# One gate matmul per token tile, weights split and set up later, and the first batch's gathers without clearings between them

## The chip, the cores and the metric

The kernel runs on one core of one Trainium2 chip. The metric is the time of one execution on the device in microseconds; for a kernel several executions are taken and their median is given. The engines are TensorE (PE; its weight loads are shown as PEld), VectorE (DVE), ScalarE (ACT), GpSimd (POOL) and SyncE (SP), each with its own in-order queue of instructions, tied together by semaphores.

## The reference

For each of 16 images `x[b]` (64 channels, 128x128) and texts `txt[b]` (128 tokens of 64):

```python
q_feat = bilinear_sample(x, 32x32 grid)                      # 1024 queries
queries = q_feat @ W_q.T
off = gelu(layer_norm(q_feat @ W_o1 + b_o1)) @ W_o2 + b_o2   # 8 points a query
sampled = bilinear_sample(x, grid + 4 * off * scale)         # 1024 x 8 points, 4 corners each
h = softmax(q . (sampled @ W_k.T)) over the 8 points, applied to sampled @ W_v.T
h = concat([h, txt])                                         # 1152 tokens of 64
h = h + ssm(layernorm(h))       # diagonal complex recurrence over the BATCH index, 16 steps
z = layernorm(h)
logits = z @ gate_w + gate_b ; top 2 of 16 experts, softmax over the two
h = h + sum_e dispatch[e] * ((silu(z @ w1[e]) * (z @ w2[e])) @ w3[e])   # 16 experts, hidden 128
```

All 16 experts are computed for every token, and the dispatch weight of the experts not chosen is zero. Because the recurrence runs over the batch, batch b+1 needs the state of batch b.

## The kernel before

Each batch passes through three stages, and the stages of neighbouring batches overlap:

- **Map** (pieces A1 to B6). SP loads the image in 8 units; PE transposes it (A1, 16 pieces, L770), ACT copies it to `pixmaj` (L913), and SP writes it in four quarters (Q) to a table in HBM, in rows of 2 pixels by 64 channels. A2 (L783) samples the regular grid, A3 and B0 make the queries, B1 to B5 the offsets, and B6 on DVE the table indices `idx` and the corner weights `cw`. B1 needs one power on POOL (L616).
- **Gather** (G on POOL, then D1 to D5 and S1 to S3). A batch has 8 tiles of 128 queries with 8 points each, so 64 indirect gathers, in 32 units `G` of two (L601). A unit ends with a clearing of a scratch tile `rest` (L608). Two gather buffers alternate, so tile j may be gathered once tile j-2 was weighted. D1 (DVE, L1138) multiplies half a tile by the corner weights, D2 (PE, L748) sums the corners by transposing into one bank, ACT copies, D3 (PE, L758) projects to keys and values, DVE multiplies by the queries and reduces. S1 to S3 are the softmax over four tiles (`u` = 0, 1), with the large product at L1166 and three additions at L1173.
- **FFN** (P1 to P9, R, X, W, Z, M2), in three groups of 384 tokens. P1 and P5 are the layernorms (a power on POOL each, L621 and L624), P2 to P4 the recurrence step, P6 makes the transposed token tile `xsplit`, P7 the gate: logits (PE, L736), on DVE bias (L1100), maxima and indices, P8 the dispatch weights, P9 turns them. R spreads an expert pair's weight over the bank (PE, L694). X is an expert's two hidden products (PE, L658 and L659, two passes each, high and low part of the weight), silu on ACT (L842) and the product on DVE (L1038). W is the third weight (L667), scaled on DVE (L1045), and Z sums (L677).

The order of pieces on each engine is written out by hand as strings (`ORDER`), one letter a piece; every engine walks its string and waits in it. So a piece that is early in its data still waits for the pieces in front of it on its engine. Batch 0's FFN starts while the last tiles of batch 0 are gathered.

**Set-up.** SP loads 42 constants in four parts between image units 2 to 5 (`load_constants`). Among them are w3 (L554) and w1 and w2, each twice (four loads of 512 KB), into the two gather buffers as scratch. Before its first piece DVE waits for all of them, splits w1 and w2 into a high and a low part (L960, L961), then waits for four exponentials of ACT (`setup`, which ACT runs after its last map copy of batch 0), computes phases (L974 to L986), and signals `setup_done`. PE waits for that before A2 of batch 0, and POOL before its first gather. The 128x64 transposition of `b_st` (L640), its copy (L830), a sine on ACT (L832) and the rotation matrix (L989 to L991) follow; they are needed first by P2 and P3.

Of the kernel before, what the change touches and what calls it, by code (L numbers as in the profile page):

```python
# [34 lines left out]
C = 64  # L35
# [21 lines left out]
RESTS = 1  # L57
# [23 lines left out]
def grid():  # L81
# [99 lines left out]
        "DlDJIDmDJmtJluJIvJlJImJKmxJIlJzaJlIJmaBJmIDaJDlDJIDalDJaDmJDKDItmJuaJlIaJlvIJamJbmbJIbbJbbxbJKIblJzI",
        "lJcmJBmJIDdDJlDJIDeDlDJKDmDJItmJuJlIJlvhJiImJamJaIJxaJKIJzaIJaaJJaaIBJDJDIlDJKDJIDlDJmDJIDmtJluJIvJl",
        "JImJKmxJIlJzaJlIJmaBJmIDaJDlDJIDalDJaDmJDKDItmJuaJlIaJlvIJamJbmbJIbbbJbxbJKIblJzIlJcmJBmJIDdDJlDJIDe",
        "DlDJmDJKDItmJuJlIJvlhJIimJImJaJxaJaKIJzIaJaJaJaIaBJDJDIDlDJKDJIDlDJmDJItmuJlvJIJlJImJxmJKIlJzaJlIJma",
        "BJmIDaJDlDJIDalDJaDmJDKDItmJuaJlIaJlvIJamJbmbJIbbbJbxbJKIblJzIlJcmJBmJIDdDJlDJIDeDlDJmDJKDItmJuJlIJl",
        "vhJiImJamJaIJxaJKIJzaIJaaJJaaIBJDJDIlDJKDJIDlDJmDJIDmtJluJvIJlJImJKmxJIlJzaJlIJmaBJmIDaJDlIDJaDlJDam",
        "DJKDIDmtJauJlIaJlvIJamJbmbJIbbbJbxbJKIblJzIlJcmJBmJIDdDJlDJIDeDlDJmDJKDItmJuJlIJlvhJiImJamJaIJxaJKIJ",
        "zaIJaJaJaaIBJDJDIlDJKDJIDlDJmDJIDmtJluJIvJlJImJKmxJIlJzaJlIJmaBJmIDaJDlDIDJaDlJDamDJKDItmJuaJlIaJlvI",
        "JamJbmbJIbbbJbxbJKIblJzIlJcmJBmJIDdDJlDJIDeDlDJKDmDJItmJuJlIJlvhJiImJamJaIJxaJKIJzaIJaJaJaaIBJDJDIDl",
        "DJKDJIDlDJmDJItmuJlvJIJlJImJKmxJIlJzaJlIJmaBJmIDaJDlDJIDalDJaDmJDKDItmJuaJlIaJlvIJamJbmbJIbbbJbxbJKI",  # L190
        "blJzIlJcmJBmJIDdDJlDJIDeDlDJmDJKDItmJuJlIJlvhJiImJamJaIJxaJKIJzaIJaJaJaaIBJDJDIDlDJKDJIDlDJmDJItmuJl",
        "vJIJlJImJKmxJIlJzaJlIJmaBJmIDaJDlDJIDalDJaDmJDKDItmJuaJlIaJlvIJamJbmbJIbbbJbxbJKIblJzIlJcmJBmJIDdDJl",
        "DJIDeDlDJKDmDJItmJuJlIJlvhJiImJamJaIJxaJKIJzaIJaaJJaaIBJDJDIlDJKDJIDlDJmDJIDmtJluJIvJlJImJKmxJIlJzaJ",
        "lIJmaBJmIDaJDlDIDJaDlJDamDJKDItmJuaJlIaJlvIJamJbmbJIbbbJbxbJKIblJzIlJcmJBmJIDdDJlDJIDeDlDJmDJKDItmJu",
        "JlIJvlhJIimJImJJxJKIJzIJJJIBJDJDIlDJKDJIDlDJmDJIDmtJluJIvJlJImJKmxJIlJzIJlJmJIBmDJlDJIDlDJmDJKDIDmDJ",
        "ItJluJlvIJmJmJIJxJKIlJzIlJmJmJIBJlDJIDlDJmDJKDIDmDJlDJItJluJIvmJImJKJxIJzJJIJJIBJDJDIJDKDJIDJIDJDJDI",
        "tJuJIvJKJIJxJIzJJIJBJDJDIJDKDJIDJIDJDJDItJuJIvJKJIxJJzIJJIJBJDIDJKDJIDJDJDIDJDJIJJIJKJIJJIJJIJIK",
    ),
    "act": (
        "aaaaaaaaaaaaaaaabcdghaaaaaaaalmmaaalammlmamaaablcmdmEglmhmsltamumaawaalxamJmzJaJaBaDJDJaDJlDmDJmDJaD",  # L200
        "JEDJaJalamJsmJJtulJwmJmxJzJaJBaslDJmDJmDJDJDJDJlDJmDmtJuEJwlbJmcJmdxJzlJmBJsmDJDDJDDJDlDJmDJgtmuJhJw",
        "JlJmamaJxaJEJaJaJzaJaaBJDsJDDDJDJDlDJmDJtmuJJJwlJmJxmJJaJzlJmaBJmDsaDJDDJaDlJDamDJDtmJuaJEaJlJamwJmJ",
# [55 lines left out]
        "oosoooooowoooooosoowswsw",  # L258
    ),
    "sp": (  # L260
        "ppHHppCppCppCppCppCppCppCppCpppppCCpCppCrHrppCppCrppCrpHpCrppCppCrppCrpHpCrppCppCrppCrpHpCrppCppCrpp",
        "CrpHpCrppCppCrppCrpHpCrppCppCrppCrpHpCrppCppCrppCrpHpCrppCppCrppCrpHpCrppCppCrppCrpHpCrppCppCrppCrpH",
        "pCrppCppCrppCrpHpCrppCppCrppCrpHpCrppCppCrppCrHCrrrrrrrr",
    ),
# [970 lines left out]
OFF_READ = 12  # L1235
SOFT_N = 7
LN_N = 2
TOP_N = 12


# [48 lines left out]
```

## Time and profile before

| | us |
|---|---|
| median of 3 runs | 2207.96 (2207.76 to 2212.83) |
| the profiled execution | 2205.73 |
| its span | 2203.9 |
| PE busy in the span | 2028.7 (92%) |
| DVE busy | 1775.4 (81%) |
| POOL busy | 1513.4 (69%) |
| ACT busy | 1184.9 (54%) |
| mean granted clock of TensorE | 0.977 |

The profile is that of one execution; its own time is 2205.73 us, and the runs of the table's first line are others. The share of busy time of an engine is a mean over stages with different limits. In the slices of the page PE is at 2 to 8 tenths in the first four of 40 slices (55 us each) and at 9 in nearly all that follow.

### The profile page before, as it was taken

The numbers are of one execution on the slowest core, as the hardware profiler recorded it, in microseconds if no ns is written. First come the engines' busy times: TensorE is split into PE (matmuls) and PEld (weight loads), VectorE is DVE, ScalarE is ACT, GpSimd is POOL, SyncE is SP. The second block draws the span as 40 slices with busy tenths as digits, with TensorE's granted clock in tenths as the row PEclk, the third lists the DMA queues.
The fourth block names the chain that finished last, engine by engine and source line by source line (L and its number), as shares of the span: only waits on it lengthen the run. The fifth ranks groups of instructions, "written<-read, shape, count | busy, mean of one in ns | idle before, by whom it ended". The sixth has DMA issues, their size and how long they took to land.

```text
span 2203.9 us, 42639 instructions
## 1 busy us (share of the span) xinstructions
PE 2028.7 (92%) x13857; PEld 1541.3 (70%) x13857; DVE 1775.4 (81%) x4292; ACT 1184.9 (54%) x3048; POOL 1513.4 (69%) x1753
## 2 busy tenths in 40 slices
PE   2468999999999999999999999999999999999998
PEld 1346677777777777777777777777777677776765
DVE  1346788888889888888988888898988889898875
ACT  1225555555565555655555565555556556654553
POOL 0378778778686867868676786868688686868700
PEclk9778999999999999999999999999999999999999
DMA  8786726667654656656464666646476664632200
GB/s 196 218 240 171 214 74 186 178 179 197 168 156 116 188 161 186 195 165 174 121 192 133 188 197 172 184 121 194 119 201 176 179 191 126 184 95 75 71 3 6
DMA packets 363274, 346.61 MB, mean 157 GB/s; under 512 B 49456, under 2 KB 313776, under 8 KB 362928
## 3 DMA queue, kind: packets, MB, share of 16 engines
q1 hardware_dynamic: 313904, 209.60, 34.9%
q0 software_dynamic: 49152, 134.28, 21.0%
q8 instruction: 114, 1.87, 0.4%
q14 instruction: 104, 0.85, 0.1%
HBM read 205.90 MB, written 137.89 MB: 156 GB/s over the span
## 4 chain that ended last, share of the span: by engine, by line
PE 67%; DVE 12%; POOL 10%; issue 8%; ACT 2%; DMA 1%; POOLq 0%; DVEq 0%; ACTq 0%; SPq 0%
PE bank_h L658 11%; PE bank_o L667 10%; PE bank_h L659 9%; PE bank_d L748 9%; PE bank_d L758 9%; POOL gath L601 7%; PE bank_z L677 4%; PE bank_p L694 4%; PE bank_a L770 2%; DVE hid L1038 2%; DVE v_sb L1166 2%; DVE v_sb L1173 2%; PE bank_p L713 2%; PE bank_p L718 1%; POOL rest L608 1%
## 5 line engine op out<-in xcount | busy, mean ns | idle before, releaser
L601 POOL DMA_INDIRECT gath<-table,idx x1024 | 1133.9, 1107 | 258.5 <-issue 239.8
L658 PE MATMUL bank_h<-xsplit,w 128*128 128x384 f32 x1536 | 587.5, 382 | 18.7 <-DVE hid L1038 17.5
L659 PE MATMUL bank_h<-xsplit,w 128*128 128x384 f32 x1536 | 521.1, 339 | 0.0
L842 ACT ACTIVATE silu<-bank_h 128x384 f32<-128x384 f32 x768 | 382.5, 498 | 241.7 <-PE bank_h L659 239.7
L1038 DVE TENSOR_TENSOR hid<-silu,bank_h 128x384 f32<-128x384 f32 x768 | 419.9, 550 | 82.0 <-ACT silu L842 74.0
L658 PEld LDWEIGHTS bank_h<-xsplit,w 128*128 128x128 f32 x1536 | 293.0, 191 | 118.8 <-issue 63.8
L1138 DVE TENSOR_TENSOR wsam<-gath,cw 128x1024 f32<-128x1024 f32 x256 | 313.0, 1223 | 53.0 <-PE bank_d L748 27.0
L667 PE MATMUL bank_o<-hid,w_sb 128*64 128x384 f32 x1536 | 334.7, 514 | 12.2 <-DVE scaled L1045 10.8
L748 PE MATMUL bank_d<-eye,wsam 128*128 128x128 f32 x2048 | 275.7, 279 | 25.3 <-DVE wsam L1138 24.8
L659 PEld LDWEIGHTS bank_h<-xsplit,w 128*128 128x128 f32 x1536 | 293.7, 191 | 3.2
L758 PE MATMUL bank_d<-w_kv,samT 128*128 128x256 f32 x1024 | 278.5, 395 | 5.6 <-ACT v_sb L898 2.7
L748 PEld LDWEIGHTS bank_d<-eye,wsam 128*128 128x128 f32 x2048 | 237.5, 143 | 63.0 <-DVE wsam L1138 41.9
L882 ACT COPY wide<-bank_p 128x384 f32<-128x384 f32 x384 | 185.0, 482 | 161.8 <-PE bank_p L694 161.2
L770 PE MATMUL bank_a<-eye,xin 128*128 128x128 f32 x1024 | 171.4, 294 | 76.9 <-DMA xin<-x_dram 43.4
L621 POOL TENSOR_SCALAR lns<-lns 128x3 f32<-128x3 f32 x96 | 39.1, 408 | 293.4 <-ACT lnsq L848 289.4
L913 ACT COPY pixmaj<-bank_a 128x512 f32<-128x512 f32 x256 | 150.2, 587 | 139.9 <-PE bank_a L770 137.6
L1045 DVE TENSOR_TENSOR scaled<-bank_o,wide 128x384 f32<-128x384 f32 x384 | 212.2, 553 | 12.2 <-PE bank_o L667 8.1
L758 PEld LDWEIGHTS bank_d<-w_kv,samT 128*128 128x128 f32 x1024 | 181.3, 193 | 51.8 <-issue 22.1
L608 POOL MEMSET rest<- 1x400 f32 x512 | 215.9, 422 | 0.2
L770 PEld LDWEIGHTS bank_a<-eye,xin 128*128 128x128 f32 x1024 | 127.2, 149 | 114.7 <-issue 56.3
L1144 DVE TENSOR_TENSOR k_sb<-k_sb,q_sb 128x256 f32<-128x256 f32 x256 | 108.3, 423 | 114.8 <-ACT v_sb L898 114.0
L894 ACT COPY k_sb<-bank_d 128x256 f32<-128x256 f32 x256 | 95.3, 372 | 156.1 <-PE bank_d L758 155.0
(157 smaller groups left out, 2704.4 us busy)
## 6 DMA issues: line engine op xcount, KB each, us to landing
table<-pixmaj SPq DMA_DIRECT2D x80, 1024.0 KB, 9.7
xin<-x_dram SPq DMA_DIRECT2D x256, 256.0 KB
table<-pixmaj SPq DMA_DIRECT2D x32, 960.0 KB
table<-pixmaj SPq DMA_DIRECT2D x16, 1088.0 KB
gath<-table,idx POOLq DMA_INDIRECT x1024
out_dram<-ob SPq DMA_DIRECT2D x48, 96.0 KB, 7.0
gath<-w_dram SPq DMA_DIRECT2D x4, 512.0 KB, 9.5
interp_sb<-interp_dram SPq DMA_DIRECT2D x1, 1024.0 KB, 5.2
```

Of the source, the lines that this page charges most:

```text
L601: pool.indirect_dma_start(out=gath[buf][:, p, :, :].rearrange("p a c -> p (a c)"), out_offset=None, in_=table[par], in_offset=bass.Indirec ...
L608: nc.gpsimd.memset(rest[:], 0.0).then_inc(rested, 1)
L658: mm(bank[:, 0:GC], w12[:, e, which, 0, :], xsplit[gp][:], start=True, stop=False)
L659: mm(bank[:, 0:GC], w12[:, e, which, 1, :], xsplit[gp][:], start=False, stop=True).then_inc(ready, 1)
L667: last = mm(bank_o[C * h:C * (h + 1), 0:GC], w3_sb[:, 2 * q + h, :], hid[:, (2 * n + h) % HB, :], start=True, stop=True)
L748: last = mm(bank_d[:, 128 * (2 * f + pair):128 * (2 * f + pair + 1)], wsam[:, corner, 2 * pair:2 * pair + 2, :].rearrange("p n c -> p (n c)"),
L758: last = mm(bank_d[:, 256 * i:256 * (i + 1)], samT[:, 2 * f + i, :], w_kv[:], start=True, stop=True)
L770: last = mm(bank_a[:, 128 * r:128 * (r + 1)], xin[u % 2][:, HW * (4 * (c % 2) + r):HW * (4 * (c % 2) + r + 1)], eye[:], start=True, stop=T ...
L842: nc.scalar.activation(silu[e % 2][:], bank_h[r][:, 0:GC], ACT.Silu).then_inc(silu_done, 1)
L1038: tt(hid[:, n % HB, :], silu[e % 2][:], bank_h[r][:, 0:GC], ALU.mult).then_inc(hid_done, 1)
L1045: tt(scaled[n % SB][:], bank_o[:, 0:GC], wide[:, q, :], ALU.mult).then_inc(eo_scaled, 1)
L1138: tt(wsam[:].rearrange("p a n c -> p n a c"), gath[j % GB][:, 4 * f:4 * f + 4, :, :], spread(w, 3, C), ALU.mult).then_inc(weighted, 1)
```

## The change

Four things are changed, and the order strings with them (2896, 2240, 2480, 624 and 256 pieces on PE, ACT, DVE, POOL and SP as before; the set of pieces is the same).

1. **Gate.** `gate_r` holds the high and the low part of the gate weights. Before, a token tile was multiplied by each with 16 columns, the second adding into the bank (6 matmuls a group). Now it is multiplied once by both, side by side (3 matmuls of 32 columns), and DVE adds the two halves in an instruction of its own.
2. **Weights.** w3 and the raw w1 and w2 are no longer among the constants. SP issues them (7 loads) right behind the last table quarter of batch 0, into the FFN tiles `wide` and `hid`; w2 is split in two halves. DVE splits them in three steps (`split_weights`) in front of D1 pieces (1,1), (2,0) and (2,1) of batch 0. The constants are now 37 in four parts.
3. **Set-up.** ACT runs the exponentials after its first samples copy (D2 of tile 0), the g_in copy and the sine after that of tile 1; DVE computes the phases in front of D1 (1,0) and the rotation in front of D1 (3,0); PE transposes `b_st` in front of D2 (1,1). A2 waits for the constants alone, and the first gather no longer for `setup_done`.
4. **Gathers.** A unit of batch 0 ends without clearing `rest`; the units of the other batches clear it as before.

Order: POOL's string begins with B1 and all 32 units of batch 0 with P1 of group 0 in front of the last; then B1 of batch 1, the first unit of batch 1, P5 of group 0. Before, B1 of batch 1 stood after unit 20, P1 after 25 and P5 after 29. On DVE S1 and S2 of the last tiles now stand in front of P6n, and S3 in front of P6 of group 0; before, they stood nine expert products later. On PE all D2 and D3 of batch 0 stand in front of the first expert, before two of its tiles' pieces stood behind it. Later batches differ in single swaps.

```diff
     "pool": (
-        "eooooooooooooooooooooeooooosoooowooooooooooooosooowoooosooooooowooooosooeooowooooooosooooowoooooosoooo",
...
+        "eooooooooooooooooooooooooooooooosoeowoooosoooooowooooosooooooowoooooosooeowooooooosoooooowoooooosooo",
...
-            (gate_f[0:C, :], gate_w), (gate_f[C:128, :], gate_w), (w3_sb[:], w3.rearrange("e h o -> h e o")),
+            (gate_f[0:C, :], gate_w), (gate_f[C:128, :], gate_w),
...
-        raw_w = [gath[0][:].rearrange("p a b c -> p (a b c)"), gath[1][:].rearrange("p a b c -> p (a b c)")]
+        flat = wide[:].rearrange("p a b -> p (a b)")
+        raw_w = [(0, 0, NE, flat[:, 0:NE * HID]), (1, 0, NE // 2, flat[:, NE * HID:NE * HID * 3 // 2]),
+                 (1, NE // 2, NE, hid[:].rearrange("p a b -> p (a b)")[:, 0:NE // 2 * HID])]
...
-            loads += [(dst, src, raw_in) for dst, src in raw_loads]
...
                         table_quarter(b, par, args[0])
+                        if b == 0 and args[0] == 3:
+                            for dst, src in raw_loads:
+                                sp.dma_start(dst, src).then_inc(raw_in, 16)
...
-                if k == 0 and b == 0:
-                    pool.wait_ge(setup_done, 1)
...
-                for n in range(RESTS * (4 * QT * b + k), RESTS * (4 * QT * b + k + 1)):
+                if b > 0:
+                    n = 4 * QT * (b - 1) + k
                     wait(pool, rested, n)
                     nc.gpsimd.memset(rest[:], 0.0).then_inc(rested, 1)
...
+                        if n == 0:
+                            pe.wait_ge(split_v, 2 * len(raw_w))
...
+                        if n == 0:
+                            pe.wait_ge(raw_in, 16 * (2 * len(raw_w) + 1))
...
-                            for part in range(2):
-                                last = mm(bank_p[:, NE * k:NE * (k + 1)], xsplit[gp][:, 128 * k:128 * (k + 1)],
-                                          gate_r[:, part, :], start=part == 0, stop=part == 1)
+                            last = mm(bank_p[:, 2 * NE * k:2 * NE * (k + 1)], xsplit[gp][:, 128 * k:128 * (k + 1)],
+                                      gate_r[:].rearrange("p a e -> p (a e)"), start=True, stop=True)
...
+                        if b == 0 and (j, f) == (1, 1):
+                            setup()
...
-                                setup()
+                                pe.wait_ge(const_in, N_CONST)
...
+                        if b == 0 and j == 0:
+                            setup()
+                        if b == 0 and j == 1:
+                            setup_state()
...
+            def split_weights(n):
+
+                which, first, last, raw = raw_w[n]
+                raw = raw.rearrange("p (e h) -> p e h", h=HID)
+                high = w12[:, first:last, which, 0, :]
+                if n == 0:
+                    dve.wait_ge(raw_in, 16 * (2 * len(raw_w) + 1))
+                vcopy(high, raw).then_inc(split_v, 1)
+                dve.wait_ge(split_v, 2 * n + 1)
+                tt(w12[:, first:last, which, 1, :], raw, high.bitcast(F32), ALU.subtract).then_inc(split_v, 1)
...
-                        link(top, tt(logit[:], bank_p[:, 0:GT * NE].rearrange("p (k e) -> p k e", k=GT),
-                                     spread(gateb[:], 1, GT), ALU.add))
+                        parts = bank_p[:, 0:2 * GT * NE].rearrange("p (k a e) -> p k a e", k=GT, a=2)
+                        link(top, tt(logit[:], parts[:, :, 0, :], spread(gateb[:], 1, GT), ALU.add))
+                        link(top, tt(logit[:], parts[:, :, 1, :], logit[:], ALU.add))
...
+                        if b == 0:
+                            if (j, f) == (1, 0):
+                                setup_phases()
+                            elif (j, f) == (3, 0):
+                                setup_rot()
+                            elif (j, f) in ((1, 1), (2, 0), (2, 1)):
+                                split_weights(2 * j + f - 3)
```

## Rows read from the trace of the kernel before

**Rows 1.** Stretches: window, length, busy PE, PEld, DVE, ACT, POOL, clock, DMA.

```profile
196.20:335.10 138.90, 128.65 (x870) 96.58 (x869) 116.81 (x279) 78.64 (x202) 107.54 (x128) 0.99 0.59 165
462.40:1988.60 1526.20, 1481.49 (x10369) 1138.53 (x10368) 1318.38 (x3193) 881.38 (x2274) 1137.95 (x1309) 0.99 0.59 167
```

**Rows 2.** What PE waited for, 335.1 to 1988.6 us: total, times, longest.

```profile
PE bank_a L770 <- ACT pixmaj L913: 13.0, 17, 0.8
PE bank_h L658 <- DVE hid L1038: 12.1, 28, 1.7
PE bank_p L684 <- DVE dispr L1127: 10.1, 12, 0.9
```

**Rows 3.** SP's issues in order of time: start, length, engine, line, what.

```profile
11.56 0.59 SPq L554 DMA_DIRECT2D w_sb<-w_dram  x1
12.19 2.23 SPq L554 DMA_DIRECT2D b_st<-bmat_dram  x1
...
24.22 2.93 SPq L554 DMA_DIRECT2D d_row<-dvec_dram  x1
27.19 7.40 SPq L554 DMA_DIRECT2D gath<-w_dram  x4
34.63 4.27 SPq L554 DMA_DIRECT2D w_off<-w_o_dram  x5
...
68.67 4.62 SPq L534 DMA_DIRECT2D table<-pixmaj  x2
91.64 1.12 SPq L519 DMA_DIRECT2D xin<-x_dram  x2
```

**Rows 4.** The set-up chain to the first gather, in order of time.

```profile
67.53 0.58 ACT L913 COPY pixmaj<-bank_a 128x512 f32<-128x512 f32 x1 [1.27 <-PE bank_a L770]
...
68.59 0.23 DVE L974 TENSOR_SCALAR col<-col 128x2 f32<-128x2 f32 x1 [8.20 <-ACT col L828]
...
71.94 3.23 PE L783 MATMUL bank_a<-pixmaj,interp_sb 128*32 128x64 f32 x128
...
82.36 1.65 POOL L616 TENSOR_TENSOR off_s<-off_s,neghalf 128x8 f32<-128x8 f32 x1 [80.78 <-DVE off_s L1189]
...
90.56 1.24 POOL L601 DMA_INDIRECT gath<-table,idx  x1 [6.56 <-DVE idx L1218]
```

**Rows 5.** DMA engines from 75 to 92 us: busy tenths, 39 slices.

```profile
DMA  9999998310000000000000000000000000000000
```

**Rows 6.** POOL: groups from 90.5 to 199.3 us, then single instructions.

```profile
L601 POOL DMA_INDIRECT gath<-table,idx x64 | 69.8, 1091 | 21.4 <-issue 14.7 <-DVE idx L1218 6.6 <-DVE wsam L1138 0.2
L608 POOL MEMSET rest<- 1x400 f32 x32 | 13.5, 422 | 0.0
...
93.64 0.95 POOL L601 DMA_INDIRECT gath<-table,idx  x1 [0.16 <-issue]
94.89 0.94 POOL L601 DMA_INDIRECT gath<-table,idx  x1 [0.30 <-issue]
...
155.68 1.68 POOL L616 TENSOR_TENSOR off_s<-off_s,neghalf 128x8 f32<-128x8 f32 x1 [6.03 <-DVE off_s L1189]
...
199.86 0.95 POOL L601 DMA_INDIRECT gath<-table,idx  x1 [0.16 <-issue]
```

**Rows 7.** A gather beside a DVE product, and the weight split's operations.

```profile
161.22 2.23 DVE L1166 TENSOR_TENSOR v_sb<-v_sb,score 128x2048 f32<-128x2048 f32 x1
161.68 2.58 POOL L601 DMA_INDIRECT gath<-table,idx  x1 [0.30 <-issue]
...
49.72 1.23 DVE L960 CAST w<-gath 128x2048 fp32r<-128x2048 f32 x1
50.98 2.29 DVE L961 TENSOR_TENSOR w<-gath,w 128x2048 fp32r<-128x2048 f32 x1
```

**Rows 8.** First silu; and the chain from D2 of the last tile to S3.

```profile
196.81 0.49 ACT L842 ACTIVATE silu<-bank_h 128x384 f32<-128x384 f32 x1
...
206.63 0.87 PE bank_d L748 x8
...
223.47 0.43 DVE v_sb L1173
```

**Rows 9.** Gate matmuls from 462.4 to 1988.6 us; the bias addition, whole span.

```profile
L736 PE MATMUL bank_p<-gate_r,xsplit 128*128 128x16 f32 x216 | 26.3, 242 | 0.0
...
L1100 DVE TENSOR_TENSOR logit<-bank_p,gateb 128x48 f32<-128x48 f32 x48 | 9.7, 202 | 2.2 <-PE bank_p L736 2.1
```

More of the change, by code:

```diff
@@ L194 @@
[L194 to L197, printed above, removed]
+        "aaaaaaaaaaaaaaaabbbbbbbbcdehiaaaallamamaallmmalaaalmmllmmlalamamabbbbbbbblcdlemmllmmltuvhilammaaaxaa",
@@ L410, in build @@
         raw_in = sem("raw_in")
+        split_v = sem("split_v")
         setup_v = sem("setup_v")
@@ L540, in out_group @@
                              ob[gp][:]).then_inc(out_done[gp], 16)
-            raw_loads = [(raw_w[n][C * half:C * (half + 1), :].rearrange("c (e h) -> c e h", e=NE),
-                          w.rearrange("e c h -> c e h")) for n, w in enumerate((w1, w2)) for half in range(2)]
+            raw_loads = [(raw[C * half:C * (half + 1), :].rearrange("c (e h) -> c e h", h=HID),
+                          (w1, w2)[which][first:last].rearrange("e c h -> c e h"))
+                         for which, first, last, raw in raw_w for half in range(2)]
+            raw_loads.append((w3_sb[:], w3.rearrange("e h o -> h e o")))
             loads = [(dst, src, const_in) for dst, src in const_loads]
-            loads += [(dst, src, raw_in) for dst, src in raw_loads]
             loads += [(dst, src, const_in) for dst, src in block_loads]
@@ L955, in _ @@
             step(nc.vector.memset(state[:], 0.0))
-            dve.wait_ge(raw_in, 64)
-            for n in range(2):
-                raw = raw_w[n].rearrange("p (e h) -> p e h", e=NE)
-                step(vcopy(w12[:, :, n, 0, :], raw))
-                step(tt(w12[:, :, n, 1, :], raw, w12[:, :, n, 0, :].bitcast(F32), ALU.subtract))
             step(vcopy(sel[:].rearrange("p (e c) -> p e c", c=C), spread(lnsq[:, 0, 0:NE], 2, C)))
@@ L979, in _ @@
-            for op, sign in ((ALU.is_gt, -1.0), (ALU.is_lt, 1.0)):
-                step(ts(col[:, 18:20], col[:, 16:18], -sign * PI, sign * TWO_PI, op, ALU.mult))
-                step(tt(col[:, 16:18], col[:, 16:18], col[:, 18:20], ALU.add))
-            step(ts(col[:, 16:18], col[:, 16:18], -PI, PI, ALU.max, ALU.min))
-            assert su.n == PHASES_READY
-            step(tt(col[:, 8:9], col[:, 6:7], col[:, 12:13], ALU.mult))
-            step(ts(b_st[:], b_st[:], col[:, 6:7], None, ALU.mult))
@@ L1112, in run @@
                         g = args[0]
-                        top.start(b, TOP_N * g + 4)
+                        top.start(b, TOP_N * g + 5)
                         dve.wait_ge(gap_tanh, NGRP * b + g + 1)
@@ L1228, in _ @@
             run()
-PHASES_READY = 29
-SETUP_V = 35
+PHASES_READY = 25
+SETUP_V = 31
 OFF_N = 20
@@ L1237 @@
 LN_N = 2
-TOP_N = 12
+TOP_N = 13
 def kernel(**inputs):
```

203 lines of the change are left out of this document (106 added, 97 removed).

## The prediction

> **What bounds the kernel now.** The views were read in this order: busy shares by stretch, PE's waits, SP's queue at the start, the chain of set-up, then POOL. In [rows 1] the reader is to see two regimes. From 462.4 to 1988.6 us PE is busy for 1481.5 of 1526.2 us, at the full granted clock but for short stretches; these are twelve batches, counted from one's last silu to another's, of 127.2 us each. There a microsecond of PE work removed is worth up to a microsecond, and the 2.9% of idle time is mostly PE waiting for DVE results or map copies [rows 2]. Before 196 us PE is mostly idle: it waits for the map, the table and the gathers of batch 0. There only the chain SP, then set-up, then POOL counts, up to the first expert matmul at about 195 us (its silu starts at 196.81 [rows 8]).
>
> **1. Earlier loads: -9.8 us on the map's arrival.** SP issues without a pause until its last table quarter, so what leaves its queue moves everything behind it. Out go the w3 load (0.59), the four raw weight loads (7.40), and what the 2.23 us of b_st exceeds an ordinary load by, since it stands right behind w3's small packets (2.23 - 0.5 = 1.7) [rows 3]: 9.7, with one w_off load moved a quarter earlier and gamma a quarter later making about nothing by the sixth unit; I take 9.8. Ends: if raw's 7.40 us was mostly SP held back by the table quarter before it, only 4 x 0.6 = 2.4 of it is work, and the gain is 2.4 + 0.6 + 1.7 = 4.7 us. If in turn the w_off loads (4.27 for five, 0.85 each) were held back by raw, it is 12 us. What moves: seven loads (2.5 MB) are now issued behind quarter 3, which ends at 68.67 + 4.62 = 73.3; SP's next issue waited until 91.64 [rows 3]. At 1.85 us each (7.40/4) they take 13 us of that gap of 18, so they delay nothing; without that cover x units 2 and 3 of batch 1 would be late by the overshoot, and no gather. They land before DVE asks for them at its fourth product, some 15 us after the gathers begin.
>
> **2. Set-up off the chain: -3.8 us.** In [rows 4] DVE stands idle until ACT's exponentials at 68.59, then works through the phases, and PE's A2 starts only at 71.94. ACT's last map copy ends at about 68.1 (67.53 + 0.58, and the exponentials follow right on it), so A2 may start at 68.1: 3.8 us. The small projections and B6 behind it are untouched and end in the first gather at 90.56. The moved pieces cost DVE some 4 us (14 small operations of 0.17 to 0.25) and ACT a Sin table load, inside the gather phase of batch 0, where DVE is about half idle and the gathers run two tiles ahead of it; I cost them at nothing, at most 3 us if DVE becomes late for a gather buffer. The first gather thus comes at 90.6 - 9.8 - 3.8 = 77.0 us. The table is not late: the DMA engines fall quiet by 80 us [rows 5], some 10 before the first gather, and that point moves by 9.8 against 13.6.
>
> **3. POOL's phase of batch 0.** Today the 64 gathers take from 90.56 to 199.3 [rows 6]. The 32 clearings look like 13.5 us, but the gap in front of a gather is 0.16 after a clearing and 0.30 after a gather, so a unit goes from 0.95 + 0.30 + 0.95 + 0.42 + 0.16 = 2.78 to 2 x (0.95 + 0.30) = 2.50: 0.28 x 32 = 9.0 us. The order also changes: B1 of batch 1, for which POOL stood idle 6.03 us and worked 1.7 (8 us), now follows the last gather, and only P1 of group 0 remains inside (1.6 us; P5, 2.4 us, moves out).
>
> Against it stands a loss. A gather normally takes 0.95 us; some of the 64 take longer, 9.0 us in all (69.8 - 64 x 0.95), and in [rows 7] one that starts inside DVE's 2.23 us product lasts 2.58 and ends 0.8 us after it. The six weight splits that the change puts between D1 pieces last 1.23 + 2.29 + as much again in halves = 7.0 us [rows 7]. A gather waits on average for what is left of the operation beyond its own place in the 1.25 us rhythm; I take 4 us, between 0 (if every split falls between two gathers) and 7.0. That makes 80.0 + 1.6 + 9 + 4 = 94.6 us, so the last gather ends at 171.6, 28 us earlier than now.
>
> The Trainium skill, "SBUF — State Buffer", section "Who interferes with whom", says that a DVE operation with two inputs in SBUF and a GpSimd instruction that reads SBUF shut each other out for the whole instruction, and that one that only writes (the clearing) is not held. The trace agrees on both: 2.58 us beside 2.23 for a gather, and clearings at a mean of 422 ns throughout [rows 6, 7]. By it the splits would cost up to their 7 us, 3 more than my sum.
>
> **4. But the first expert matmul gains almost nothing.** POOL's order now makes the chain serial. Behind the last gather stand B1 (0.3 + 8.2 us from B1 to the gather that needs its result, as 82.36 to 90.56 [rows 4]), and one D1 of 1.2 in the middle of it: batch 1's gathers start at 181.5, 18 us earlier than 199.9 [rows 6]. P5 of group 0 stands behind them. On DVE, P6 of group 0 now stands behind D1, S1, S2 and S3 of the last tiles. From D2 of that tile to the end of S3 the chain today takes 206.63 to 223.9 = 17.3 us [rows 8]. The last D2 starts at 171.6 + 6.7 (B1, B2 and B4, then D1 of 1.2), S3 ends at 195.6, P6 and the gate add 1.0: the first expert matmul at 196.6, against about 195.1. So 28 us on POOL turn into -1.5 us here.
>
> What the delay buys: D3 of tile 6 and all of D2/D3 of tile 7 lie before the first expert matmul now, some 5.3 us of PE work (five pieces; a D2 is 0.87 [rows 8], and I estimate a D3, whose four matmuls are twice as wide, at a fifth more), and the gathers of batch 1 are 18 us ahead, so of PE's 10.3 idle us between 196.2 and 335.1 [rows 1], half of which waits on weighted samples, I take 5 as gone. Sum of the beginning: 9.8 and 3.8 and the rest have gone into POOL's lead, and what the end sees is -1.5 + 5.3 + 5.0 = 8.8 us. It ranges from -4 (every late term at its bad end: 5 us less at SP, 3 at POOL, 5.0 not gained) to 25 (S1 to S3 in 12 us as DVE is freer, loads 12 us).
>
> **5. One-pass gate: -9.6 us.** The six matmuls of a group occupy PE for 26.3 us/216 = 0.122 us each [rows 9]; 48 groups lose three each: 144 x 0.122 = 17.5 us if 32 columns cost no more than 16. The nearest row is weight loads of the same 128x128 shape, which set this rhythm and are halved; at the other end, a matmul twice as long would leave 0. DVE gains 48 additions of the size of L1100 (0.20 us [rows 9] and 0.03 of hand-over): 11 us on an engine that is busy 86% of this stretch. PE waits for the dispatch 12 times and for hidden products 28 times in 39 groups [rows 2]; there the added 0.23 us eats most of the 0.37. I take 0.20 kept per group, 9.6 us; range -3 to 17.5. Other moves in the order strings (B0 a few places later, single swaps) I cost at nothing, +-2.
>
> **Sum.** The profiled execution took 2205.7 us (span 2203.9 and 1.8 around it). 8.8 + 9.6 = 18.4: 2187.3. The median of the runs is 2208.0, 2.3 above the profiled one, so the forecast for a median is 2189.6, as **2189 us**.
>
> **Rivals.**
> - *The lead survives.* DVE, freed of the FFN's early pieces, gets through D1 to S3 faster, or PE fills the gap; the end sees 18 of POOL's 28 us, and the gate brings 15: 2208 - 33 = 2175. For it: PE's idle share before 196 us is the largest reserve. Against it: the fixed order on POOL and DVE.
> - *The gate gives nothing.* The chain through DVE (addition, maxima, indices, P8, dispatch) sets the pace, or 32 columns cost double; only the beginning counts: 2208 - 9 = 2199. For it: the DVE waits in [rows 2]. Against: they are 2% of the stretch.
> - *Little of either.* 2205.
> - *Slower: the first FFN starts late.* Place: POOL's queue, B1 and P5 of batch 0 behind all 32 units, and P6 behind S3. Price: each microsecond of lateness of the last gather is one of the whole. Decides from a first expert matmul at 195.1 + 5.3 + 5 + 9.6 = 215 us on. It needs SP's gain at its low end (5), the splits at 7, and gathers that wait for late D1 pieces (10): 196.6 + 5 + 3 + 10 = 214.6, and the gate at its bad end: 2208 + 9 = 2217.
>
> **Chances.** Forecast 0.50 (own range 2181 to 2197), lead survives 0.20, gate gives nothing 0.16, little of either 0.08, slower 0.06. The range 2171 to 2203 leaves out the slower case and part of the next. The chance of being faster by over 0.3% (below 2201.4; 0.3% is about what a measurement of this kernel tells from no change) is 0.86, within it 0.08, slower 0.06.
>
> **What would show it.** First gather near 77 us and A2 right behind the last map copy (steps 1, 2); gather rhythm 2.50 us and the last one near 172 (3); longer gathers beside the splits; batch 1's gathers near 181 and the first silu near 198 (4); L736's successor with 144 matmuls, and a period between silus of one batch and the next of 126.5 instead of 127.1 (5). A first silu before 190 or after 208, or a period unchanged to 0.1 us, would prove me wrong.

## The result, and the profile after

| | before | after |
|---|---|---|
| median, 5 runs each | 2207.96 us (2206.97 to 2213.07) | 2193.04 us (2188.33 to 2194.95) |
| profiled execution | 2205.73, span 2203.9 | 2190.43, span 2188.6 |
| mean granted clock in it | 0.977 | 0.969 |

The ratio of the two is 0.992, 95% interval 0.9902 to 0.9939: faster by 0.8%, 14.9 us by the medians and 15.3 us by the profiled executions. The forecast was 2189 us, range 2171 to 2203. In every ratio of this document an execution that took over 1.5% longer than the fastest of its kernel is left out as a slow one (in this comparison there is none).

Where the 15.3 us arose is read from the start of the last silu of each batch. That of batch 0 comes at 322.6 instead of 335.1 us (-12.5), of batch 12 at 1844.9 instead of 1861.7 (-16.8), of batch 13 at 1971.1 instead of 1988.6 (-17.5), of batch 15 at 2181.3 instead of 2196.6 (-15.3). So most of it is won by the end of batch 0, a few us in the steady batches, and 2 us are lost again at the end.

The busy shares by stretch, with the columns of [rows 1]: the phase of the first gathers, the stretch up to the first expert matmul, batch 0's FFN, and the same twelve batches as before, from the last silu of batch 1 to that of batch 13.

```profile
75.40:166.20 90.80, 55.71 (x376) 42.36 (x377) 47.72 (x79) 26.92 (x66) 71.50 (x67) 0.73 0.87 239
166.20:196.30 30.10, 21.32 (x72) 14.15 (x72) 19.62 (x44) 8.63 (x25) 13.34 (x14) 0.56 0.30 72
196.30:322.60 126.30, 120.76 (x838) 92.77 (x839) 104.60 (x272) 74.53 (x193) 96.55 (x113) 0.99 0.61 172
449.40:1971.10 1521.70, 1475.05 (x10262) 1127.50 (x10261) 1319.14 (x3229) 881.12 (x2275) 1138.84 (x1309) 0.99 0.60 167
```

Against [rows 1] batch 0's FFN has 7.9 us less PE work (128.65 to 120.76) and 4.8 us less idle (10.3 to 5.5). By the rows of single lines in the same windows, 16 of D2's and 12 of D3's matmuls have gone from it (20.26 to 17.79 and 20.48 to 17.05 us, together 5.9), and half of the gate's (2.40 to 1.45). The twelve batches take 1521.7 us where they took 1526.2: 126.8 against 127.2 a batch. PE's work fell by 6.4 us and its idle time rose by 1.9. What it waited for from the end of batch 0 on (322.6 to 1971.1 us, thirteen batches; total, times, longest), against [rows 2]: the hidden product now comes first, and the wait for map copies has grown from 13.0 to 16.9 us.

```profile
PE bank_h L665 <- DVE hid L1064: 17.5, 24, 1.7
PE bank_a L780 <- ACT pixmaj L930: 16.9, 22, 0.8
PE bank_p L693 <- DVE dispr L1154: 7.7, 10, 0.9
```

SP's queue, against [rows 3]: start and length of each issue.

```profile
11.55 0.59 SPq L557 DMA_DIRECT2D b_st<-bmat_dram  x1
...
16.84 3.11 SPq L536 DMA_DIRECT2D table<-pixmaj  x2
19.99 4.53 SPq L557 DMA_DIRECT2D col<-gamma_dram  x2
24.56 0.59 SPq L557 DMA_DIRECT2D d_row<-dvec_dram  x1
25.20 2.74 SPq L557 DMA_DIRECT2D w_off<-w_o_dram  x6
...
57.16 4.72 SPq L536 DMA_DIRECT2D table<-pixmaj  x2
61.93 6.92 SPq L572 DMA_DIRECT2D wide<-w_dram  x4
68.91 3.02 SPq L572 DMA_DIRECT2D hid<-w_dram  x2
71.97 1.23 SPq L572 DMA_DIRECT2D w_sb<-w_dram  x1
76.51 2.19 SPq L521 DMA_DIRECT2D xin<-x_dram  x2
```

The last table quarter is issued at 57.16 instead of 68.67, 11.5 us earlier. b_st costs 0.59 instead of 2.23 us, six w_off loads 2.74 where five took 4.27, but two tiny gamma loads behind a table quarter 4.53. The seven late loads end at 73.2, before SP's next issue at 76.51.

The set-up chain, against [rows 4]: A2 (L793) begins right behind the last map copy, and the first gather at 75.43 instead of 90.56.

```profile
56.02 0.59 ACT L930 COPY pixmaj<-bank_a 128x512 f32<-128x512 f32 x1 [1.27 <-PE bank_a L780]
...
56.75 3.32 PE L793 MATMUL bank_a<-pixmaj,interp_sb 128*32 128x64 f32 x128 [0.77 <-ACT pixmaj L930]
...
67.21 1.66 POOL L621 TENSOR_TENSOR off_s<-off_s,neghalf 128x8 f32<-128x8 f32 x1 [65.64 <-DVE off_s L1223]
...
75.43 1.24 POOL L605 DMA_INDIRECT gath<-table,idx  x1 [6.56 <-DVE idx L1252]
```

In the gather phase, the first step of the weight split on DVE (its two operations, L1017 and L1019) and the gathers beside it, against [rows 7]:

```profile
103.33 1.22 DVE L1017 CAST w<-wide 128x2048 fp32r<-128x2048 f32 x1
104.58 2.29 DVE L1019 TENSOR_TENSOR w<-wide,w 128x2048 fp32r<-128x2048 f32 x1
106.79 1.22 DVE L1172 TENSOR_TENSOR wsam<-gath,cw 128x1024 f32<-128x1024 f32 x1
```

```profile
102.14 1.03 POOL L605 DMA_INDIRECT gath<-table,idx  x1 [0.30 <-issue]
103.48 1.89 POOL L605 DMA_INDIRECT gath<-table,idx  x1 [0.30 <-issue]
105.67 2.03 POOL L605 DMA_INDIRECT gath<-table,idx  x1 [0.30 <-issue]
108.00 1.43 POOL L605 DMA_INDIRECT gath<-table,idx  x1 [0.30 <-issue]
```

A gather in the clear takes 0.95 us and the next follows 0.30 later. Three here are 2.5 us longer in sum. Of all 64, what exceeds 0.95 us comes to 9.7 us, against 9.1 in the kernel before; 2.9 of the 9.7 fall on the four that run beside an operation of the split (at 103.48, 105.67, 108.00 and 117.55 us).

From the last gather to the first silu, against [rows 6, 8]:

```profile
165.13 0.95 POOL L605 DMA_INDIRECT gath<-table,idx  x1 [0.30 <-issue]
166.12 1.80 POOL L621 TENSOR_TENSOR off_s<-off_s,neghalf 128x8 f32<-128x8 f32 x1
180.03 1.07 POOL L605 DMA_INDIRECT gath<-table,idx  x1 [12.12 <-DVE idx L1252]
```

```profile
175.21 1.22 DVE L1172 TENSOR_TENSOR wsam<-gath,cw 128x1024 f32<-128x1024 f32 x1
...
189.11 2.23 DVE L1200 TENSOR_TENSOR v_sb<-v_sb,score 128x2048 f32<-128x2048 f32 x1
...
191.72 2.40 DVE L1207 TENSOR_TENSOR v_sb<-v_sb 128x1024 f32<-128x1024 f32 x3
...
194.62 0.56 DVE L1120 TENSOR_TENSOR xsplit<-bank_p,xsplit 64x384 fp32r<-64x384 f32 x1
...
196.30 0.67 PE L665 MATMUL bank_h<-xsplit,w 128*128 128x384 f32 x1
...
197.94 0.49 ACT L855 ACTIVATE silu<-bank_h 128x384 f32<-128x384 f32 x1
```

The last gather ends at 166.1 (199.3 before), yet the first silu comes at 197.94 (196.81 before): the lead of 33 us on POOL is spent in the serial chain of B1, the last D1, S1 to S3 and P6. Before, the first silu did not wait for the last gather: it came 2.5 us ahead of the gather's end.

The gate in the twelve batches, against [rows 9]:

```profile
L744 PE MATMUL bank_p<-gate_r,xsplit 128*128 128x32 f32 x108 | 14.4, 234 | 0.0
L1128 DVE TENSOR_TENSOR logit<-bank_p,logit 128x48 f32<-128x48 f32 x36 | 7.5, 208 | 1.2
```

216 matmuls of 16 columns in 26.3 us have become 108 of 32 in 14.4: 0.122 and 0.133 us each. So 32 columns cost hardly more than 16, and PE gave up 11.9 us of gate. Its total fell by only 6.4.

### The profile page after: what moved, and what is told of

Read it like the earlier page. It is cut to its first block, busy times and chain, and to the rows that moved or that the text cites. A ratio compares the mean times of both kernels' runs of the same rounds, so it can differ in the third digit from the quotient of the medians.

```text
span 2188.6 us, 42370 instructions
## 1 busy us (share of the span) xinstructions
PE 2022.5 (92%) x13713; PEld 1529.3 (70%) x13713; DVE 1778.0 (81%) x4342; ACT 1182.0 (54%) x3046; POOL 1504.3 (69%) x1721
## 4 chain that ended last, share of the span: by engine, by line
PE 72%; DVE 11%; POOL 7%; issue 7%; ACT 3%; DMA 1%; POOLq 0%; DVEq 0%; SPq 0%; ACTq 0%
PE bank_h L665 11%; PE bank_o L676 11%; PE bank_d L758 10%; PE bank_h L666 10%; PE bank_d L768 10%; POOL gath L605 5%; PE bank_z L686 4%; PE bank_p L703 4%; PE bank_a L780 3%; DVE hid L1064 2%; PE bank_p L722 2%; DVE v_sb L1200 2%; PE bank_p L721 1%; PE bank_a L793 1%; PE bank_p L727 1%
## 5 line engine op out<-in xcount | busy, mean ns | idle before, releaser
L1172 DVE TENSOR_TENSOR wsam<-gath,cw 128x1024 f32<-128x1024 f32 x256 | 312.8, 1222 | 56.7 <-PE bank_d L758 36.9
L626 POOL TENSOR_SCALAR lns<-lns 128x3 f32<-128x3 f32 x96 | 45.5, 474 | 297.4 <-ACT lnsq L861 293.9
L613 POOL MEMSET rest<- 1x400 f32 x480 | 202.4, 422 | 0.2
## 6 DMA issues: line engine op xcount, KB each, us to landing
table<-pixmaj SPq DMA_DIRECT2D x80, 1024.0 KB, 12.5
```

The costliest lines, as they stand in the source:

```text
L613: nc.gpsimd.memset(rest[:], 0.0).then_inc(rested, 1)
L1172: tt(wsam[:].rearrange("p a n c -> p n a c"), gath[j % GB][:, 4 * f:4 * f + 4, :, :], spread(w, 3, C), ALU.mult).then_inc(weighted, 1)
```

## The experiments

Eight kernels ran in three sets (twelve entries in all), each set on another chip and with the kernel before on the same one. Which chip the comparison above ran on is not known; it is called the first chip below, and taken for a fourth by its times. In the sets every kernel, the one before included, took about 12% longer with a much wider scatter. So absolute times below stand beside medians of 2472, 2467 and 2477 us for the kernel before, not beside 2208. The "mean" is over all executions of a kernel (standard error behind it). In set 2 the ratio of the beginning rests on 2 of its 12 executions and says little. The kernel before was profiled on the first chip alone.

| kernel | mean, us | less than before there | ratio (95%) | mean clock |
|---|---|---|---|---|
| before, set 1 / 2 / 3 | 2474.0 / 2469.7 / 2480.1 (2.4 / 2.3 / 2.0) | | 1 | 0.943 / 0.942 / 0.941 |
| gate alone, set 1 | 2451.2 (3.5) | 22.8 | 0.990 (0.986 to 0.993) | 0.950 |
| gate alone, set 2 | 2445.1 (4.3) | 24.6 | 0.992 (0.988 to 0.996) | 0.950 |
| gate alone, set 3 | 2452.4 (3.9) | 27.7 | 0.987 (0.983 to 0.991) | 0.948 |
| beginning alone, set 1 | 2460.4 (5.0) | 13.6 | 0.996 (0.992 to 1.001) | 0.938 |
| beginning alone, set 2 | 2453.1 (4.2) | 16.6 | 0.985 (0.978 to 0.992), of two executions | 0.939 |
| beginning alone, set 3 | 2468.5 (4.6) | 11.6 | 0.997 (0.993 to 1.000) | 0.937 |
| the changed kernel, set 3 | 2462.9 (2.4) | 17.2 | 0.995 (0.992 to 0.998) | 0.944 |
| clearings back, set 1 | 2447.0 (5.0) | 27.0 | 0.989 (0.984 to 0.994) | 0.951 |
| second addition left out, set 1 | 2442.8 (3.4) | 31.2 | 0.988 (0.984 to 0.992) | 0.945 |
| FFN pieces earlier, set 2 | 2444.1 (4.4) | 25.6 | 0.989 (0.985 to 0.994) | 0.945 |
| splits twice, set 2 | 2449.3 (4.4) | 20.4 | 0.992 (0.988 to 0.997) | 0.945 |
| raw weights early, set 3 | 2472.8 (3.3) | 7.3 | 0.997 (0.994 to 1.001) | 0.943 |

**e1, f1, g2: the gate alone.** The kernel before with this edit (lines abridged):

```diff
-for part in range(2):
-    last = mm(bank_p[:, NE*k:NE*(k+1)], xsplit[gp][:, ...], gate_r[:, part, :], start=part == 0, stop=part == 1)
+last = mm(bank_p[:, 2*NE*k:2*NE*(k+1)], xsplit[gp][:, ...], gate_r as 2*NE columns, start=True, stop=True)
-link(top, tt(logit[:], bank_p, gateb, ALU.add))
+link(top, tt(logit[:], parts[:, :, 0, :], gateb, ALU.add)); link(top, tt(logit[:], parts[:, :, 1, :], logit[:], ALU.add))
```

> The kernel before with the one-pass gate alone (3 matmuls of 32 columns a group, one more DVE addition); order strings, loads, set-up and clearings as before. My theory: the gate is worth 0.2 us a group and shows as a batch period shorter by 0.4 to 0.6 us; 2208 - 8 = 2200, with the beginning (last silu of batch 0 at 335) unchanged. Rival A (the DVE addition eats it all, or 32 columns cost double): 2208, period 127.2. Rival B (all 0.37 us a group are kept): 2190.

> The same kernel as e1_gate_only (before with the one-pass gate alone), once more, since on the chip of the first set every kernel took 12% longer. On a chip like that of the first profiles my theory expects 2200 (gate worth 0.2 us a group, -8), rival A 2208 (nothing), rival B 2190 (all of the 17.5 us of matmuls, as the ratio 0.990 of the first set would have it).

> The kernel before with only the one-pass gate. My theory: it keeps the 5 to 10 us of the steady batches (0.10 to 0.20 us a group, 48 groups) and none of the beginning's: 0.9955 to 0.998 on a chip like the first (2198 to 2203 us of 2208), mean batch distance 126.6 to 126.9 against 127.2, first silu at 196.8. Rival (the gate carries all of it): 0.992. On a chip of 2470 us it gave 0.990 and 0.992 before, so there I expect 0.991.

Measured: 22.8, 24.6 and 27.7 us less than before. The direction is firm, the size is not what the theory of PE time gives: 144 matmuls fewer, and the 144 that remain wider, are at most 17.5 us by [rows 9], so even rival B is passed. Part of the rest goes with the clock. The mean granted clock of these runs is 0.948 to 0.950 against 0.941 to 0.943. With two levels, full and half, a mean of 0.949 is 2 x 0.051 x 2450 = 250 us at half clock, and 0.942 is 2 x 0.058 x 2475 = 287 us. Where PE is busy, each of these 37 us can cost up to half of itself, 18 us. Whether the shorter gate lets the clock stay up or a freer kernel merely has a higher mean, these runs don't tell.

**e2, f2, g3: the beginning alone.** The changed kernel with the gate in two passes (the edit above, reversed); the later batches keep its order strings.

> The changed kernel with the gate of before (6 matmuls of 16 columns a group, one DVE addition), all else as changed. My theory: the beginning alone is left, 2208 - 9 to 12 = 2197 to 2199, last silu of batch 0 at 323, period 127.2. Rival (the gate gave nothing, all of the gain is the beginning): 2193, as the changed kernel.

> The same kernel as e2_two_pass (changed, with the gate of before), once more. My theory (the beginning alone is worth 9 to 12 us): 2197 to 2199, last silu of batch 0 near 323 us, first silu near 198. Rival (the gate gave nothing): 2193.

> The changed kernel with the gate in two passes as before: the beginning alone. My theory: first gather 75.4, last silu of batch 0 near 324 (12 us less 1 for the gate), batch distance 127.1: 0.9945 to 0.996 on a chip like the first. Rival (the beginning's gain is given back in the steady batches, or was the gate's): 0.999 to 1. On a chip of 2470 us it was 0.996 and 0.985, which does not tell the two apart; a value there between them, 0.992, would put gate and beginning at the same worth.

Measured: 13.6, 16.6 and 11.6 us less than before, at the lowest clock of all (0.937 to 0.939). The two parts don't add: 25 and 14 alone, 17 (+-3) together in set 3, the only one that has the changed kernel itself. The traces show that the beginning brings batch 0 nothing there beside the gate alone. In all three the first gather starts at 74.8 to 76.5 us as on the first chip, but the first silu comes at 224.8, 215.7 and 221.4 us, against 203.1, 205.0 and 204.3 for the gate alone; the last silu of batch 0 at 365.5, 357.5 and 361.9 against 362.3, 363.0 and 362.1. So a beginning that goes with 12.5 us less at this place on the first chip ends batch 0 hardly earlier than the old beginning with the new gate (361.6 against 362.5 us on the mean). Where its 14 us in the whole time come from is open, since there is no profile of the kernel before in these sets. One kernel's profiles also differ by up to 9.1 us at the first silu and 8.0 at batch 0's end.

**g1: the changed kernel itself.**

> The changed kernel itself, unaltered, on the same chip as the three beside it. My theory: on a chip like that of the first comparison its ratio to the kernel before is 0.992 again, and its first gather starts near 75.4 us, the first silu near 198 us, the last silu of batch 0 near 322.6 and the mean distance of one batch's last silu to the next one's is 126.8. Rival (the change's worth is a property of the chip): on a chip where all kernels take 2470 us, as in the first eight experiments, the first silu comes at 215 to 230 us, some 20 us later than in the kernel before there, the last silu of batch 0 is at 358 to 380, no earlier than the 362 of the kernel with only the gate changed, and the ratio is 0.985 to 0.992, set by the steady batches.

Measured: 17.2 us less than before; first silu at 223.2, last silu of batch 0 at 370.8. So the rival held for the places in the trace: the gain of the beginning at batch 0's end belongs to the conditions of the first chip. Its ratio of 0.985 to 0.992 did not come: it was 0.995 (0.992 to 0.998). On this chip the changed kernel is also slower than the gate alone, 2462.9 (2.4) against 2452.4 (3.9) us, with ratios of 0.995 and 0.987 whose intervals don't meet. So there the other changes took back part of what the gate had gained. POOL's gathers of batch 0 (75 to 182 us) in this kernel, then the first gather of batch 1:

```profile
L605 POOL DMA_INDIRECT gath<-table,idx x64 | 66.0, 1031 | 43.4 <-DVE wsam L1172 19.6 <-issue 17.3 <-DVE idx L1252 6.6
```

```profile
206.87 1.02 POOL L605 DMA_INDIRECT gath<-table,idx  x1 [22.71 <-DVE idx L1252]
```

On the first chip no gather of this phase waited for D1 (L1172); here they do for 19.6 us, since D1 pieces are late, and the serial chain behind them is longer too (22.71 idle where it was 12.12). One thing that makes D1 late is a pause of DVE ahead of it, for something the profile has no name for ("remote"): 4.67 us in this phase (first row), and 4.71 in a steady batch, where PE waits 4.98 us for it.

```profile
172.91 1.22 DVE L1172 TENSOR_TENSOR wsam<-gath,cw 128x1024 f32<-128x1024 f32 x1 [4.67 <-remote]
...
1021.27 0.56 DVE L1071 TENSOR_TENSOR scaled<-bank_o,wide 128x384 f32<-128x384 f32 x1
1026.54 1.23 DVE L1172 TENSOR_TENSOR wsam<-gath,cw 128x1024 f32<-128x1024 f32 x1 [4.71 <-remote]
```

```profile
1027.82 1.97 PE L758 MATMUL bank_d<-eye,wsam 128*128 128x128 f32 x8 [4.98 <-DVE wsam L1172]
```

The operations themselves last what they did (D1 1.23, a clear gather 0.95). What has grown are such pauses (behind batch 0, those over 1.5 us come to 209 us on ACT and 87 on DVE, and the first chip's profile has none), and the time at half clock: the eight D2 matmuls behind the pause take 1.97 us at a clock of 0.50, where eight take 1.09 at full clock. Twelve steady batches of this kernel there (columns of [rows 1]):

```profile
515.00:2235.00 1720.00, 1545.63 (x10254) 1156.59 (x10253) 1323.03 (x3222) 884.59 (x2272) 1108.76 (x1304) 0.97 0.52 148
```

PE is idle for 174 of 1720 us where it was for 47 of 1522, and 71 us busier for the same matmuls. In the DVE pauses over 0.6 us ahead of a D1 the last packet of the gathered data had ended 9.3 us earlier at the median (over all 54 behind 200 us; 31 of these were released by PE, and for the 18 "remote" ones the median is 11.6), and a fetch of instructions ended within only 10 of DVE's 29 pauses over 2.5 us behind batch 0. So late data doesn't account for them, and code loading not for most; what does is open.

**g4: the raw weights early.** In the changed kernel the seven late loads go back among the early ones:

```diff
 loads = [(dst, src, const_in) for dst, src in const_loads]
+loads += [(dst, src, raw_in) for dst, src in raw_loads]
 loads += [(dst, src, const_in) for dst, src in block_loads]
...
-if b == 0 and args[0] == 3:
-    for dst, src in raw_loads:
-        sp.dma_start(dst, src).then_inc(raw_in, 16)
```

> The changed kernel with its seven late loads (raw w1 and w2 in six pieces, w3) issued where the kernel before has its raw ones, ahead of the block weights; everything else as changed. My theory (step 1 of the prediction, each microsecond of SP before the last table quarter delays the map and the first gather): seven loads of 0.6 to 1.85 us each bring the last table quarter 8 to 12 us later, the first gather at 83 to 87 us instead of 75.4, and the first silu and the last silu of batch 0 later by as much: 0.3 to 0.5% longer than the changed kernel. Rival (SP has slack, or the map waits for something else by now): first gather within 2 us of 75.4, and the same time.

Measured, on the same chip as g1: 9.9 us (+-4) longer than the changed kernel by the means; the intervals of the two ratios (0.997 and 0.995) overlap. SP's rows, g4's, then the changed kernel's there:

```profile
25.43 5.04 SPq L558 DMA_DIRECT2D wide<-w_dram  x3
30.52 1.96 SPq L558 DMA_DIRECT2D hid<-w_dram  x2
32.52 1.16 SPq L558 DMA_DIRECT2D w_sb<-w_dram  x1
33.72 7.02 SPq L558 DMA_DIRECT2D w_off<-w_o_dram  x5
...
70.46 4.90 SPq L536 DMA_DIRECT2D table<-pixmaj  x2
```

```profile
26.63 2.27 SPq L557 DMA_DIRECT2D w_off<-w_o_dram  x5
...
58.03 4.80 SPq L536 DMA_DIRECT2D table<-pixmaj  x2
```

The last table quarter comes 12.4 us later, the first gather 12.2 (88.53 against 76.28), the first silu 15.8 (239.0 against 223.2), the last silu of batch 0 15.0 (385.8 against 370.8). This is the cleanest result of the study: what leaves SP's queue ahead of the table comes back in full at the first gather, whose start differs by only 1.8 us among three profiles of one kernel (the beginning alone). Here it also shows at the end of batch 0, though one profile of each kernel, at a place where one kernel's profiles differ by 8.0 us, doesn't give its size. It also sizes the mechanism: five w_off loads take 7.02 us behind the raw loads and 2.27 without them.

**e3: the clearings back.** In the changed kernel `if b > 0:` ahead of the clearing becomes `if b >= 0:` (and the count behind it follows).

> The changed kernel with the clearings of the scratch tile back behind each unit of batch 0. My theory: a unit takes 2.78 us instead of 2.50, the last gather ends 8 to 9 us later (at 175 instead of 166.1), and since POOL's queue is serial with the first expert, the first silu comes 5 to 9 us later than 197.9 and the whole is 5 to 8 us longer than the changed kernel, 2198 to 2201. Rival (the lead of POOL was not what the end sees, the chain through DVE or PE sets the first expert): first silu moved by under 2 us, 2193.

Measured: no cost is seen (27.0 us less than before; the changed kernel itself is not in this set). POOL's gathers and clearings from 75 to 180 us:

```profile
L605 POOL DMA_INDIRECT gath<-table,idx x64 | 69.0, 1078 | 25.9 <-issue 14.6 <-DVE idx L1252 6.6 <-DVE wsam L1172 4.7
L613 POOL MEMSET rest<- 1x400 f32 x32 | 14.0, 437 | 0.0
```

The 14.0 us of clearings are there, and the wait for D1 has shrunk from 19.6 to 4.7 us (g1's row). The phase lasts 103.0 us (75.7 to 178.7), that of the changed kernel 104.1. On this chip POOL had slack to fill. On the first chip no gather of the changed kernel waited for D1 in this phase, so there the clearings should cost their 9 us; that wasn't measured.

**e4: the second addition left out.** The logits then lack the product with the low part of the gate weights.

```diff
-link(top, tt(logit[:], parts[:, :, 1, :], logit[:], ALU.add))
```

> The changed kernel without the second addition of the logits: the part that comes from the low half of the gate weights is left out of them, so a logit has the precision of the high half alone. My theory: the addition (0.23 us in DVE's chain, 48 times) costs up to 0.1 to 0.2 us a group; 2193 - 5 = 2188, period 126.5 instead of 126.8. Rival (PE alone sets the pace, DVE's addition is free): 2193, period 126.8.

Measured: 2442.8 (3.4) us, the least of all, beside 2447.0 (5.0) for e3 in the same set. It can't be told from the other kernels with the new gate. A cost of the 48 additions of more than some 10 us is unlikely; more these runs don't say.

**f4: the splits twice.** Each of the three steps of the weight split in front of D1 is done two times (abridged; PE waits for twice the count).

```diff
-vcopy(high, raw).then_inc(split_v, 1)
-dve.wait_ge(split_v, 2 * n + 1)
-tt(w12[...], raw, high.bitcast(F32), ALU.subtract).then_inc(split_v, 1)
+for again in range(2):
+    the same two operations, each waiting for the one before
```

> The changed kernel with each weight split done twice (six more DVE operations, 7 us, between the same D1 pieces). Theory of the lock, by the gathers' durations: those gathers that start beside a split lose 4 us for 7 us of splits, so a second set lengthens the gather phase of batch 0 (75.4 to 166.1 us) by 4 us. Rival (the gathers run two tiles ahead and only D1's lateness counts): longer gathers are few and the phase ends within 1 us of 166.1. The whole: 2193 to 2197.

Measured: what the 64 gathers take beyond 0.95 us each is 8.8 us; in the seven other kernels there that have the new beginning and no clearings it is 4.7 to 6.6, mean 5.4. So 7.0 us of splits more cost gathers 3.4 us, near the theory's 4. The phase however takes 112.1 us against 104 (100.1 to 106.3), twice the theory's 4: the rest is waiting, since gathers wait 22.8 us for D1 here and 13.8 to 21.7 in the others. So the rival, D1's lateness, counts as well. In the whole time (2449.3) it is lost in the scatter.

**f3: pieces of batch 0's FFN earlier.** A reordering at the border, in the order strings alone: P6 of group 0 ahead of the last S3, P5, P7 and the first X some places earlier on POOL, DVE, PE and ACT.

> The changed kernel with 14 pieces moved at the border of batch 0: on POOL P5 of group 0 stands before batch 1's first gather, on DVE P5 before B6 and P6n, P6 and the first experts before S2 and S3, on PE and ACT P6, P7 and the first expert before three map pieces. My theory (the queue order at that border holds the first expert, POOL's 28 us lead is lost there): first silu at 185 to 190 instead of 197.9, and since PE then starts its backlog earlier, the whole is 5 to 9 us shorter, 2184 to 2188. Rival (the beginning is set by PE's and DVE's total work and not by the order; S2 and S3 only come later): first silu earlier, but last silu of batch 0 unmoved at 322 and the whole 2193.

Measured: first silu at 220.3 us, no earlier than in the others there (215.7 to 224.8), and the last silu of batch 0 at 382.8, the second latest of all; this profile is of an execution of 2460.7 us, 17 above the kernel's mean. The serial chain wasn't seen to shorten by the order alone on this chip; the whole time is 25.6 us less than before, within the scatter of its siblings.

## Why the prediction was right, step by step

The sum (-18.4) came out as -15.3 in the profiled executions, by a larger beginning and a smaller gate. Part of that is luck: at batch 0's end 12.5 us were won where 9.4 stood, and behind it 2.8 where 9.0 stood, two misses of 3.1 and 6.2 us that partly cancel. Gate and beginning were run apart only in the three sets, so what is said of each here is read from places in one trace of each kernel. The upper end of the beginning's range, 25, doesn't follow from the two cases named for it, which give 8.8 + 5.3 + 2.2 = 16.3.

1. **Earlier loads, -9.8.** Measured 11.5 at SP's last quarter. The high end of the step's range, w_off held back by the raw loads, was nearly the case: on a slower chip g4 shows 7.02 against 2.27 us. The hold behind the first table quarter only moved, from d_row (2.93 us, now 0.59) to the two gamma loads (4.53, in the kernel before 1.24 behind others). That the late loads delay nothing held: they end at 73.2, before SP's next issue at 76.51.
2. **Set-up, -3.8.** A2 starts at 56.75 for 71.94, 15.2 earlier, of which 11.5 are the loads: 3.7. First gather at 75.43, forecast 77.0.
3. **POOL's phase, 94.6 us.** Measured 90.7 (75.4 to 166.1). The rhythm is 1.25 a gather as forecast. What was too large is the surplus of the gathers, 9 + 4 = 13 forecast and 9.7 measured. The gathers beside the splits have 2.9 of it, where 4 stood (f4's price of 0.5 us per us of split gives 3.4). The others have 6.8, where the forecast kept the 9.0 of the kernel before, though the phase became 18 us shorter. By "SBUF — State Buffer" of the Trainium skill, "Who interferes with whom", a gather is shut out for as long as such an operation lasts, which the prediction put at up to 7 us for the splits. The trace agrees with the rule for single gathers (2.03 us across a split of 2.29), and not with that sum.
4. **The chain is serial.** First silu at 197.94, forecast 198, for a lead of POOL that was 33 instead of 28 us: the last D1 started 9.1 us behind the last gather, forecast 5.5 (6.7 less D1's own 1.2), and P6 (194.62) 19.4 behind that D1, forecast 18.5 (1.2 + 17.3), so 4.5 of the 5.5 us more of lead went into the chain. B1 and the way to batch 1's first gather took 13.9 us, forecast 9.9. PE's work in batch 0's FFN fell by 7.9 us: 1.0 of gate (2.40 to 1.45), 5.9 of D2 and D3 moved ahead, forecast 5.3, and 1.0 that isn't assigned. Idle time fell by 4.8, forecast 5.0. With the first silu 1.1 later that is -11.6; the rest of the -12.5 is that the window of [rows 1] begins 1 us behind the first expert matmul of the kernel before (195.23) and not of the one after. Forecast were 8.8, and 0.6 of gate.
5. **Gate, -9.6.** This term was too large, as a net. The matmuls cost what was assumed (0.133 us at 32 columns, 0.122 at 16): 11.9 us were saved in the twelve batches. Of it 4.5 us reached the end of them. Idle time ate 1.9: in thirteen batches the wait for hidden products went from 12.1 to 17.5 us and that for map copies from 13.0 to 16.9, though that for the dispatch fell from 10.1 to 7.7. The period became 126.8 us, forecast 126.5. The other 5.5 us are PE work that grew elsewhere. What the trace shows to have grown is time at half clock: 16 us of these twelve batches before, 30 after, and 14 us more of it can cost up to 7. Two stretches of the kernel after, just before and in such a time at half clock (columns of [rows 1]):

```profile
1458.00:1465.00 7.00, 5.13 (x31) 3.54 (x29) 6.76 (x20) 3.65 (x9) 6.12 (x5) 1.00 0.88 230
1466.00:1472.00 6.00, 5.54 (x19) 3.63 (x18) 5.72 (x19) 2.40 (x8) 4.82 (x6) 0.50 1.09 305
```

   In 6 us at a clock of 0.50, PE is busy for 92% with 19 matmuls; in 7 us at 1.00, for 73% with 31 (the mix of matmuls is not the same). Over the runs of the kernel after, too, the time goes with the clock: 2188.33 us at 0.974, 2190.43 at 0.969, 2193.04 at 0.970, 2193.62 at 0.966, 2194.95 at 0.963. That the lower clock is a consequence of the change is not shown: of the kernel before there is one clock on the first chip (0.977). In all three sets the beginning alone has the lowest clock of all kernels (0.937 to 0.939), and the gate alone one of the highest, so if the change costs it, the beginning is the likelier part.

Of the rivals, "the gate gives nothing" was nearest on the first chip: 4.5 of the gate's 11.9 us were left in the steady batches. In the sets the opposite holds, with the gate alone worth 23 to 28 us. "The first FFN starts late" did not happen on the first chip and did in the sets: first silu at 216 to 230 us (239 with the raw weights early), where the gate alone has 203 to 205, and no clear gain over it at batch 0's end, by the place it named (gathers that wait for late D1 pieces, and what is queued behind them). The whole kernel was still faster there than the one before, and slower than with the gate alone.

## What to carry to other kernels

Follow a queue of issues by what it delays: 11.5 us out of SP's queue came back one for one at the first gather, and in g4 the loads put back cost 12.2 us there. But a lead on one engine is worth what the serial chain behind it leaves: 33 us on POOL became nothing at the first silu, and what counted was work moved under the wait (5.9 us) and less idle time in batch 0's FFN (4.8). Test a saving on more than one chip when it removes slack: here one part went with 12 us at batch 0's end on one chip, and on three others ended batch 0 hardly earlier than the kernel without it.

## What the hardware showed that was not expected

- The same kernels took 12% longer in the three sets, with unchanged operations (D1 1.23 us, a clear gather 0.95): the changed kernel's trace in set 3 has pauses of single engines, released by nothing that the profile names (behind 200 us up to 5.0 us on DVE and 6.8 on ACT), often at the same place in each batch (ACT stands idle for over 4 us ahead of its copy L934 in 11 of 16 batches, and for 2.7 at most behind batch 0 on the first chip), and 282 us at half clock where the first chip has 138.
- Two tiny loads (gamma) take 4.53 us to issue right behind a table quarter; b_st took 2.23 behind w3 and takes 0.59 elsewhere. So an issue's time on SP can be mostly that of what stands before it.
- A gather beside one large DVE product took 2.75 us at 140.90, where the product (2.23) began at 140.61: it ended 0.8 us after it, as in [rows 7].
